# A down stage that takes two short matrix products and a long one in turn, instead of twelve short ones and then six long ones

## The reference

```
q = query + braak_embed[braak_stages][..., None]
attn = softmax(einsum('bsd,btd->bst', q, key))
x1 = einsum('bst,btd->bsd', attn, value)
...
nx = x * rsqrt(mean(x * x) + EPS) * norm_w
probs = softmax(t @ gate_w.T); weights = normalised top 2 of 8 experts
h1 = t @ w1.T + SCALING * (t @ a1[e].T) @ b1[e].T
h3 = t @ w3.T + SCALING * (t @ a3[e].T) @ b3[e].T
act = silu(h1) * h3
out_e = act @ w2.T + SCALING * (act @ a2[e].T) @ b2[e].T
out = x + sum over e of weights[e] * out_e
```

## Time and profile before

| what | value |
| --- | --- |
| median of 3 runs | 1319.39 us (1318.46 to 1321.3) |
| the profiled execution | 1319.08 us, its span 1317.3 us |
| granted clock of PE | 0.998 |
| PE busy | 1307.7 us, 99% of the span |
| weight loads busy | 1144.1 us, 87% |
| DVE, ACT, POOL busy | 65%, 40%, 19% |
| chain that ended last | PE 97% |

### The profile page before, as it was taken

One profiled execution on the slowest core, in us unless ns is written; L12 is line 12 of the kernel. 1 busy time (PEld: TensorE's weight loads), 2 busy tenths in 40 slices (PEclk: granted clock), 3 DMA queues, 4 the chain that ended last, 5 costly groups with the idle time before them and its releaser, 6 DMA issues.

```text
span 1317.3 us, 18439 instructions
## 1 busy us (share of the span) xinstructions
PE 1307.7 (99%) x7280; PEld 1144.1 (87%) x7280; DVE 851.4 (65%) x1558; ACT 529.1 (40%) x990; POOL 247.3 (19%) x197
## 2 busy tenths in 40 slices
PE   8999999999999999999999999999999999999998
PEld 8999998888888888888888888888888888888887
DVE  5776656756676567756675677557665766565555
ACT  5767663333243334333333334333333343233332
POOL 2565640202011020202020202011020202020200
PEclk9999999999999999999999999999999999999999
DMA  8455810020202020100202020202020100102000
GB/s 287 126 154 163 226 53 33 2 72 1 72 2 73 0 65 8 50 25 14 60 2 73 1 72 2 73 0 73 2 72 1 57 17 25 50 1 72 1 17 16
DMA packets 73582, 69.56 MB, mean 53 GB/s; under 512 B 7050, under 2 KB 64792, under 8 KB 73368
## 3 DMA queue, kind: packets, MB, share of 16 engines
q1 hardware_dynamic: 73184, 68.37, 17.3%
q10 hardware_dynamic: 312, 0.02, 0.0%
HBM read 51.27 MB, written 17.10 MB: 52 GB/s over the span
## 4 chain that ended last, share of the span: by engine, by line
PE 97%; ACT 1%; DVE 1%; DMA 0%; issue 0%; ACTq 0%; DVEq 0%
PE bank L1152 30%; PE bank L1153 30%; PE bank L1154 30%; PE bank L1205 2%; PE bank L1278 2%; PE bank L1256 1%; PE bank L1198 1%; ACT prob L634 0%; DMA embed_in<-in_L_cond_braak_embed 0%; ACT qT_hi L617 0%; ACT kT_hi L618 0%; DVE act_br L1039 0%; DVE act_b L1036 0%; DVE br_lo L1049 0%; ACT br_hi L718 0%
## 5 line engine op out<-in xcount | busy, mean ns | idle before, releaser
L1028 DVE TENSOR_TENSOR act_a<-silu_a,bank 128x512 f32<-128x512 f32 x128 | 87.6, 685 | 250.4 <-PE bank L1154 234.5
L718 ACT ACTIVATE br_hi<-act_br 128x512 fp32r<-128x512 f32 x128 | 81.1, 633 | 188.3 <-DVE act_br L1039 188.3
L711 ACT ACTIVATE silu_b<-bank 128x512 f32<-128x512 f32 x128 | 76.2, 596 | 191.8 <-PE bank L1154 191.0
L707 ACT ACTIVATE silu_a<-bank 128x512 f32<-128x512 f32 x128 | 76.0, 594 | 175.5 <-PE bank L1154 175.4
L1154 PE MATMUL bank<-w2T_hi,s_lo 128*128 128x256 f32 x512 | 144.9, 283 | 0.0
L1153 PE MATMUL bank<-w2T_lo,s_hi 128*128 128x256 f32 x512 | 144.8, 283 | 0.0
L1152 PE MATMUL bank<-w2T_hi,s_hi 128*128 128x256 f32 x512 | 144.2, 282 | 0.0
L564 POOL TENSOR_TENSOR t_lo<-t_scaled,t_hi 128x1024 fp32r<-128x1024 f32 x16 | 38.3, 2393 | 553.9 <-ACT t_hi L699 553.9
L1036 DVE TENSOR_TENSOR act_b<-silu_b,bank 128x512 f32<-128x512 f32 x128 | 87.9, 687 | 75.7 <-PE bank L1154 74.7
L580 POOL TENSOR_TENSOR v_lo<-v_full,v_hi 128x512 fp32r<-128x512 f32 x64 | 94.4, 1508 | 139.9 <-ACT v_hi L703 139.9
L1049 DVE TENSOR_TENSOR br_lo<-act_br,br_hi 128x512 fp32r<-128x512 f32 x128 | 104.6, 817 | 5.8 <-ACT br_hi L718 3.3
(11 more groups left out here) (190 smaller groups left out, 3267.3 us busy)
## 6 DMA issues: line engine op xcount, KB each, us to landing
x_in<-in_x SPq DMA_DIRECT2D x32, 256.0 KB, 3.9
kv<-in_fside_BxSxS SPq DMA_DIRECT2D x32, 256.0 KB, 3.3
t_scratch<-oT SPq DMA_DIRECT2D x32, 256.0 KB, 2.5
t_in<-t_scratch SPq DMA_DIRECT2D x16, 512.0 KB
x_out<-in_x SPq DMA_DIRECT2D x16, 512.0 KB, 3.9
out<-x_out SPq DMA_DIRECT2D x30, 256.0 KB, 5.3
rho<-scale_scratch SPq DMA_DIRECT2D x16, 256.0 KB
rstd<-scale_scratch SPq DMA_DIRECT2D x16, 256.0 KB
```

The costliest lines, as they stand in the source:

```text
L707: nc.scalar.activation(silu_a[j % 2][:, :], h1_bank[j % 2][:, :], ACT.Silu).then_inc(silu_a_ready, 1)
L711: nc.scalar.activation(silu_b[:, :], h1_bank[j % 2][:, :], ACT.Silu).then_inc(silu_b_ready, 1)
L718: nc.scalar.activation(br_hi[j % 2][:, :], act_br[j % 2][:, :], ACT.Copy).then_inc(br_hi_ready, 1)
L1028: nc.vector.tensor_tensor(act_a[j % 2][:, :], silu_a[j % 2][:, :], h3_bank[j % 2][:, :], ALU.mult).then_inc(act_a_ready, 1)
```

## The change

A new helper `down(c, j)` issues the same eighteen products of a chunk as down_y and down_z, in another order: two short ones and a long one, six times. Short product m belongs to block m // 3 and to part m % 3 of the split; the long ones go through sa and then ba. The start flags are per block and bank as before. `pe_tile` calls it wherever down_y and down_z stood one behind the other: at the start of a tile (chunk 6 of the tile before), at j = 1 (chunk 7 of the tile before), and at j = 3 to 7 (chunks 1 to 5). Chunk 0 and the end of the last tile stay as they were. At j = 7 of a routed tile transpose_rows stood between down_y and down_z; it now stands behind the whole of `down`. Weights and moving operand are those of before, product for product.

```diff
+            def down(c, j):
+                pe.wait_ge(down_in_ready, chunk_no(c, j) + 1)
+                s, br = (s_hi[j % 2], s_lo[j % 2]), (br_hi[j % 2], br_lo[j % 2])
+                w, a = at(w2T, ALL, j), at(a2T, ALL, j)
+                parts = ((0, 0), (0, 1), (1, 0))
+                for n in range(2 * len(parts)):
+                    for m in (2 * n, 2 * n + 1):
+                        k, (p, r) = m // 3, parts[m % 3]
+                        nc.tensor.matmul(y_block(k), s[p][:, k * P:(k + 1) * P], w[r],
+                                         start=j == 0 and k % 2 == 0 and m % 3 == 0, stop=False, skip_group_check=True)
+                    dst, x_parts = ((sa_bank, s), (ba_bank, br))[n // 3]
+                    p, r = parts[n % 3]
+                    last = nc.tensor.matmul(dst[:, :], a[p], x_parts[r][:, :], start=j == 0 and n % 3 == 0,
+                                            stop=j == FC - 1 and n % 3 == 2)
+                return last
...
                     second_expert(c - 1, FC - 1)
-                    down_y(c - 1, FC - 2)
-                    down_z(c - 1, FC - 2).then_inc(down_done, 1)
+                    down(c - 1, FC - 2).then_inc(down_done, 1)
...
                     if j == 1 and not first:
-                        down_y(c - 1, FC - 1)
-                        down_z(c - 1, FC - 1).then_inc(down_done, 1)
+                        down(c - 1, FC - 1).then_inc(down_done, 1)
...
-                    elif j == 3:
-                        down_y(c, 1)
-                        down_z(c, 1).then_inc(down_done, 1)
-                    elif j >= 4:
-                        down_y(c, j - 2)
+                    elif j >= 3:
+                        last_down = down(c, j - 2)
+                        last_down.then_inc(down_done, 1)
                         if j == 7 and routes:
                             pe.wait_ge(act_b_ready, n + 7)
                             transpose_rows(group_in(c), h1_bank[0])
-                        down_z(c, j - 2).then_inc(down_done, 1)
```

## The result

| | before | changed |
| --- | --- | --- |
| median | 1319.1 us (1318.46 to 1321.3) | 1325.42 us (1325.19 to 1326.31) |
| ratio | | 1.005, 95% interval 1.0038 to 1.0062 |
| profiled execution, span | 1319.08, 1317.3 us | 1325.19, 1323.4 us |
| granted clock of PE | 0.998 | 0.998 |

The account below looks back on a forecast made before the run. PE was taken to bound the kernel. The profiled 1319.08 us plus 0 for the interleaving and 5.5 for the stall gave 1324.6, set at 1324.9 us because the profiled execution lay 0.3 below the median; range 1317.0 to 1330.0.

Parts of the forecast that it names:

- What bounds the kernel: Whole kernel: PE, busy 99% of the span and 97% of the chain, sets the time; no stretch lost to the clock.
- The transposes: At j = 7 of seven routed tiles, low_rank waits uncovered for ACT's copies: 0.79 us each, 5.5 us in all.
- X + 1.13: Forecast start of the second low_rank product in us, X being the last transpose; unstalled it would be X + 0.34.
- The wake: Time from an engine's write to PE's next load, ahead of low_rank in routed tiles: 0.05 us.
- Nobody else waits: Routed tiles: ACT's and DVE's work and SP's stores shift, but slack remains, so no second stall.
- The interleaving taken at zero: Reordered down stage, 110 chunks: bounded between 9 us gained and 8 us lost, taken as zero.
- The count: Down stage of a chunk: twelve pitches stay bound by a load and six by 512 columns, exactly as before.
- half of it: Rival, chance 0.20: first shorts quick, longs not slower; -0.045 us a chunk, -5 us, with the stall 1319.9 us.
- each change of length costs: Rival, chance 0.10: slow longs after shorts recur six times a chunk, 8 us lost, with the stall 1332.5 us.
- Loads run ahead: Rival, chance 0.12: loads start while two products lie before their own; 11 us gained over 110 chunks, with the stall 1313.9.

Follow-up runs that it names:

- The run with this part alone: Kernel before, old product order, with only the transposes of the seven routed tiles moved behind all eighteen down products: 1323.81 us against 1318.65, ratio 1.0042.
- the runs with half loads in the mixed order: Short, short, long everywhere, transposes mid-stage; weights cut from 128 to 64 columns for shorts (1319.85 us), shorts and longs (1312.62), or longs alone (1313.09).

## Why the prediction was right, point by point

- **What bounds the kernel.** Right: PE was and is the chain, and both costs are PE's. One reading was too quick: a mean of 0.998 doesn't say that no stretch was lost to the clock. The granted clock was 0.50 (1.2 GHz) from 16 to 19 us in the kernel before, behind 4 us in which PE was busy for 1.5 (12 to 16), and from 8 to 11 us in the changed one, behind 4 us in which it was busy for 2.9. From low_rank of tile 0 on it was 1.00 in both, so the comparison isn't touched.
- **The transposes.** Right in mechanism and size. The step had 0.79 us each (X + 1.13 for the second low_rank product); the trace shows 0.80 (X + 1.14). The run with this part alone has 5.2 us by the medians and 5.6 by the traces, against the forecast 5.5. The wake was 0.07 us, not 0.05. The profile put the waits down to "issue", not to scale_rows as I had written.
- **Nobody else waits.** Right: the run that only swaps the halves of low_rank keeps every other engine late and gives back the whole wait.
- **The interleaving taken at zero.** The sign was open and the bounds were -9 and +8 us; alone it costs 1.1 us by the medians, 1.5 by the traces. The count held in outcome: a chunk lost 0.10 us to its shorts before and loses 0.11 now. Its reason was too simple, so that it held is in part luck. I charged each load to the product beside it, twelve pitches one by one; the runs with half loads in the mixed order show that nothing is gained by halving the loads of the shorts, and that the long product's own costs most, part of it later, as slow longs.
- **Where its parts went.** The shorts did become a little quicker, as in the rival "half of it" (the twelve fell from 1.43 to 1.42 us; most first and second ones are at 117 to 120 ns, only the very first at 113), and the longs slower, as in the rival "each change of length costs": 229 to 241 ns, 1.41 us for six against 1.39. In whole nanoseconds of a chunk, the shorts give back 12, the six longs cost 22 and the eight pitches behind them 4: more than half of it cancels, and the 14 are left.
- **Loads run ahead.** Falsified here: in the changed kernel no load starts before the product ahead of its own, even beside a long product. The rule of the Trainium skill ("TensorE: Matmul & The Clock Gate", section "Step-by-step: what each phase is for") on loads pulled ahead of products in flight agrees with the trace for one load; that several are pulled ahead, no trace here shows.

The profiled executions differ by 6.1 us though their second parts differ by 7.0: the changed kernel's low_rank of tile 0 starts at 181.77 us and not at 182.70, since the first 21 us went quicker in that execution. The 7.0 are accounted for: 0.79 us seven times are 5.6, and 13 to 14 ns for 110 chunks are 1.5. The medians, five runs each, have 6.3.

## What to carry to other kernels

When an instruction block is moved on the engine that bounds the kernel, list what lay between each producer and the next wait on its result: six products of 1.4 us hid 0.8 us of copies and wake, and the move that laid them bare cost four to five times what the reordering itself did. Cover can be had back on either side, by putting the producer earlier or by letting the waiting stage begin with the half that doesn't need the result. Interleaving short and long products hid no loads here, where loads run one ahead. Fewer, wider products did away with their cost (12 us here), in a run that leaves out part of the result.

## What the runs showed of the hardware that I had not expected

A 512-column fp32r product is slowed (229 to 241 ns instead of 226.7) when its own 128-column weights were loaded beside a 256-column product, and several products behind it too, 28 ns in all in the kernel before; with 64-column weights it takes 226 to 230 ns. Half loads for the twelve short products alone brought 8.2 us in the old order and nothing in the mixed one. By what mechanism the delay is carried over to later products is open; no run here tells.
